# Attention over 1,024 tokens, one core: values left with channels on partitions, softmax sums inverted in a 128x16 tile and repeated by DMA, q and k stored in halves

## What is computed

```python
qkv = x @ w_qkv.T * hid ** (-0.5)
qkv = qkv.reshape(b, s, 3, heads, d)
...
scores = jnp.einsum('bhqd,bhkd->bhqk', q, k) * d ** (-0.5)
attn = jax.nn.softmax(scores, axis=-1) * (s / np.sqrt(s - 1.0))
out = jnp.einsum('bhqk,bhkd->bhqd', attn, v) * s ** (-0.5)
out = jnp.transpose(out, (0, 2, 1, 3)).reshape(b, s, hid)
return out @ w_o.T * hid ** (-0.5)
```

## Time and profile before

| | |
|---|---|
| median of 3 runs | 5755.92 us (5751.49 to 5757.47) |
| the profiled execution: time / span | 5750.62 us / 5748.9 us |
| busy in the span | PE 94%, DVE 78%, ACT 62%, POOL 26% |
| mean granted clock of TensorE | 0.976 of full speed |

### The profile page before, as it was taken

One profiled execution on the slowest core, in us unless ns is written; L12 is line 12 of the kernel. 1 busy time (PEld: TensorE's weight loads), 2 busy tenths in 40 slices (PEclk: granted clock), 3 DMA queues, 4 the chain that ended last, 5 costly groups with the idle time before them and its releaser, 6 DMA issues. The chain is left out here.

```text
span 5748.9 us, 131254 instructions
## 1 busy us (share of the span) xinstructions
PE 5428.0 (94%) x50092; PEld 3660.4 (64%) x50092; DVE 4498.2 (78%) x7377; ACT 3566.0 (62%) x5406; POOL 1473.5 (26%) x1948
## 2 busy tenths in 40 slices
PE   7999668999989889999999999999999997799999
PEld 6777457999978734444444444444444444699998
DVE  7888695555557689999999999999999996755554
ACT  5777562333325458888888888888888886433332
POOL 4655453333310000111111111111111114533332
PEclk9999889999999989999999999999999998999999
DMA  2222482222229811121112111111211113222221
GB/s 74 78 84 78 137 259 77 88 93 93 89 96 333 310 56 49 58 60 57 57 59 60 57 56 60 59 57 56 60 58 57 57 54 104 75 89 93 95 86 49
DMA packets 317697, 512.58 MB, mean 89 GB/s; under 512 B 36442, under 2 KB 221156, under 8 KB 311152
## 3 DMA queue, kind: packets, MB, share of 16 engines
q1 hardware_dynamic: 291912, 441.44, 24.2%
q0 software_dynamic: 24576, 64.56, 3.5%
q10 hardware_dynamic: 808, 1.07, 0.1%
HBM read 338.59 MB, written 185.60 MB: 91 GB/s over the span
## 5 line engine op out<-in xcount | busy, mean ns | idle before, releaser
L1773 DVE TENSOR_REDUCE at_best<-at_psM 128x2 f32<-128x1024 f32 x2048 | 2430.7, 1221 | 227.5 <-PE at_psM L1830 214.3
L1729 ACT ACTIVATE at_p<-at_psE 128x1024 f32<-128x1024 f32 (+1 forms) x2688 | 2077.1, 824 | 529.5 <-PE at_psE L1846 515.7
L1846 PE MATMUL at_psE<-at_q,at_k 50*128 50x512 f32 x4096 | 1174.0, 436 | 7.5 <-ACT at_p L1729 6.3
L1830 PE MATMUL at_psM<-at_k,at_q 48*128 48x512 f32 x4096 | 1093.6, 458 | 37.5 <-DMA at_k<-scratch_qk 27.4
L1857 PE MATMUL at_psO<-at_p,at_v 128*17 128x256 f32 x16384 | 1109.9, 383 | 0.1
L1122 ACT ACTIVATE e_h_hi<-e_psH 128x512 fp32r<-128x512 f32 x512 | 306.7, 599 | 916.0 <-PE e_psH L90 864.4
L1846 PEld LDWEIGHTS at_psE<-at_q,at_k 50*128 50x128 f32 x4096 | 548.7, 185 | 462.4 <-issue 223.6
L1196 DVE SCALAR_TENSOR_TENSOR e_h_lo<-e_psH,e_h_hi 128x512 fp32r<-128x512 f32 x512 | 353.9, 691 | 595.9 <-ACT e_h_hi L1122 505.8
L1857 PEld LDWEIGHTS at_psO<-at_p,at_v 128*17 128x17 f32 x16384 | 364.1, 96 | 542.7 <-issue 345.4
L1830 PEld LDWEIGHTS at_psM<-at_k,at_q 48*128 48x128 f32 x4096 | 471.3, 185 | 312.2 <-DVE at_best L1773 147.2
L90 PE MATMUL e_psE<-e_w_hi,e_h_hi 128*128 128x256 f32 x2048 | 583.1, 285 | 0.0
(11 more groups left out here) (213 smaller groups left out, 8456.5 us busy)
## 6 DMA issues: line engine op xcount, KB each, us to landing
e_w_raw<-in_w SPq DMA_DIRECT2D x64, 1024.0 KB
scratch_qk<-cp_qkh SPq DMA_DIRECT2D x64, 512.0 KB
scratch_qk<-cp_qkl SPq DMA_DIRECT2D x64, 512.0 KB
at_q<-scratch_qk SPq DMA_DIRECT2D x256, 128.0 KB
at_k<-scratch_qk SPq DMA_DIRECT2D x252, 128.0 KB
scratch_v<-cp_va SPq DMA_DIRECT2D x32, 544.0 KB
at_v<-scratch_v SPq DMA_DIRECT2D x126, 136.0 KB, 10.0
a_x<-in_x SPq DMA_DIRECT2D x32, 512.0 KB
```

The costliest lines, as they stand in the source:

```text
L1729: nc.scalar.activation(P[:, u:u + n, :], src, ACT.Exp, scale=HD ** -0.5).then_inc(p_ready, 1)
L1773: nc.vector.reduce_max(best[j % 2][:, h, :, qt], psM[h][:], AX_X).then_inc(m_taken, 1)
L1830: last = nc.tensor.matmul(psM[h][:, a, :], Q[j][r, 128 * qt:128 * qt + 128], K[j][r, 512 * h:512 * h + 512], start=True, stop=True)
L1846: last = nc.tensor.matmul(psE[:, u - u0 if n == 2 else 2, :], K[j][r, 128 * kc:128 * kc + 128], Q[j][r, 512 * half:512 * half + 512], star ...
```

## The change

- The DRAM tensor of q and k gets the two halves of the tokens as its first dimension. The loads of a pair take one kind of row at a time, 12 DMAs of 16 partitions where there were 8 of 32 or 16.
- `turn_values`, `normalise`, `turn_out` and `take_out` are gone. SP stores `at_oT` as it is to a DRAM tensor `scratch_ot`, moves its eight rows of sums into a tile `at_sums` of 128 x 16, DVE inverts that in place (`invert`), SP stores it (`scratch_rd`), and a unit is loaded back as 128 channels x 256 tokens (`at_raw`) beside its inverses repeated over 16 partitions (`at_den`). POOL multiplies the two before it splits.
- A unit is loaded at the start of a pair, but in pairs pb = 0 and pb = 4 behind `load_max` and `store_inverses`, since it needs the inverses of the pair just before.
- At the end of the stage the last four units are loaded with their sums repeated, inverted and multiplied on DVE.
- The PE order of a pair is written anew, and the maxima are turned at group 13 instead of 11.

```diff
@@ -1283,7 +1283,7 @@
     NG = N // G
     H, HD = 16, 16
     xg_ = x.rearrange("(b p u t) d -> u b p t d", u=2, p=128, t=4)
-    qkb = qk.rearrange("r (b h) d n -> b r (h d) n", h=H)
+    qkb = qk.rearrange("s r (b h) d n -> s b r (h d) n", h=H)
     vb = v.rearrange("b p s h k w -> s b p h k w")
     with ExitStack() as ctx:
         sb, ps, sem = tools(nc, ctx, stage)
@@ -1490,10 +1489,13 @@
     QROW, MROW = 48, 50
     NG = 21
...
+    xb = x.rearrange("(b p n) d -> b n p d", n=KC, p=128)
+    ob = out.rearrange("(b n p) d -> b n p d", n=KC, p=128)
+    qkp = qk.rearrange("s r (u a) d n -> u a r d s n", a=2)
     vp = v.rearrange("b p s (u x) k w -> u b p s (x k w)", x=2)
+    rows = ot.rearrange("(b k i) a (m w) c -> b k m (i a) w c", k=2, i=4, m=4)
+    inverses = rd.rearrange("x m i n -> x i m n")
+    inverse_rows = rd.rearrange("(b k) m i (a c) -> b k m (i a) c", k=2, a=2)
     with ExitStack() as ctx:
         sb, ps, sem = tools(nc, ctx, stage)
         Q = [sb(f"q{j}", [128, S], F32R) for j in range(4)]
...
         LEAD = 5
-        OUT_AT, MAX_AT, VALUES_AT, NORM_AT = 1, 11, 3, 3
+        OUT_AT, MAX_AT, VALUES_AT, INVERT_AT = 1, 13, 3, 11
 
...
                 r = 64 * a
-                eng.dma_start(Q[j][r:r + 32, :].bitcast(F32), row(qkp, pp)[a, 0:2]).then_inc(qk_loaded[j], 16)
-                eng.dma_start(Q[j][r + 32:r + 48, :].bitcast(F32), row(qkp, pp)[a, 0]).then_inc(qk_loaded[j], 16)
+                for n, kind in enumerate((0, 1, 0)):
+                    eng.dma_start(Q[j][r + 16 * n:r + 16 * n + 16, :].bitcast(F32), row(qkp, pp)[a, kind]).then_inc(qk_loaded[j], 16)
 
...
+            def store_values(p):
+
+                sp.wait_ge(oT_ready, p + 1)
+                T.settle(sp)
+                sp.dma_start(ot[p].rearrange("a r c -> r a c"), OT[:].rearrange("r (a c) -> r a c", a=2)).then_inc(oT_stored, 16)
+                if p < NP - 1:
+                    after(sp, rden_stored[p % 2], 16 * (p // 2))
+                    T.settle(sp)
+                    sp.dma_start(sums[p % 2][:], OT[HD:128:32, :].rearrange("q (w e) -> q w e", e=16)).then_inc(sums_moved, 16)
+
+            def store_inverses(p):
+
+                sp.wait_ge(rden_ready, p + 1)
+                T.settle(sp)
+                sp.dma_start(inverses[p // 4, p % 4], sums[p % 2][:]).then_inc(rden_stored[p % 2], 16)
+
+            def load_unit(u, slot, b, k, m, needed):
+
+                sp.wait_ge(oT_stored, 16 * needed)
+                T.settle(sp)
+                for s in range(2):
+                    sp.wait_ge(rden_stored[s], 8 * needed)
+                    T.settle(sp)
+                after(sp, ofT_ready, u - 1)
+                T.settle(sp)
+                sp.dma_start(raw[slot][:], rows[b, k, m][:, 0:HD, :]).then_inc(unit_loaded[slot], 16)
+                sp.dma_start(den[slot][:], inverse_rows[b, k, m].unsqueeze(1).broadcast_to([8, HD, 256])).then_inc(unit_loaded[slot], 16)
 
             load_queries(sp, 0, 0)
...
             def pair(pp, pb, b):
+                def next_unit():
+
+                    if has_turned(pp):
+                        u, k, m = turned_unit(pp, pb)
+                        load_unit(u, pb % 2, b if pb >= 4 else b - 1, k, m, PB * b + 4 if pb >= 4 else PB * b)
+
+                if pb % 4 > 0:
+                    next_unit()
                 if there(pp + 3):
                     after(sp, e_done, pp * NG)
                     T.settle(sp)
+                    load_queries(sp, pp + 3, (pb + 3) % 4)
+                    load_keys(sp, pp + 3, (pb + 3) % 4)
                     after(sp, pv_done, pp * KC)
                     T.settle(sp)
-                    load_pair(pp + 3, (pb + 3) % 4)
+                    load_values(sp, pp + 3, (pb + 3) % 4)
+                if not first(pp):
+                    store_values(pp - 1)
                 if there(pp + 1):
                     load_max(pp + 1, (pb + 1) % 4)
+                if not first(pp):
+                    store_inverses(pp - 1)
+                if pb % 4 == 0:
+                    next_unit()
                 if has_out(pp):
                     u, (ub, n) = out_unit(pp, pb, b)
                     store_out(u, ub, n)
             batches(pair)
+            store_values(NP - 1)
...
-                pool.wait_ge(xo_taken, u + 1)
+                pool.wait_ge(unit_loaded[slot], 32 * (u // 2 + 1))
+                T.settle(pool)
+                after(pool, xo_lo_ready, u - 1)
+                T.settle(pool)
+                nc.gpsimd.tensor_tensor(oT[slot][:], raw[slot][:], den[slot][:], ALU.mult).then_inc(ofT_ready, 1)
+                pool.wait_ge(ofT_ready, u + 1)
...
             def take_values(p):
                 act.wait_ge(pv_done, KC * p + KC)
-                after(act, t_done, p)
+                after(act, oT_stored, 16 * p)
+                after(act, sums_moved, 16 * p)
                 nc.scalar.activation(OT[:], psO[:], ACT.Copy).then_inc(oT_ready, 1)
-
-            def take_out(u, slot, bank):
-                act.wait_ge(xo_done, u + 1)
-                after(act, xo_lo_ready, u - 1)
-                nc.scalar.activation(oT[slot][:], bank[:, 128:384], ACT.Copy).then_inc(xo_taken, 1)
 
...
-            def normalise(p, pb, b):
-
-                dve.wait_ge(t_done, p + 1)
-                tv = psO[:].rearrange("p (a t w) -> p a t w", a=2, t=KC)
-                nc.vector.reciprocal(rden[:], tv[:, :, :, HD]).then_inc(rden_ready, 1)
-                dve.wait_ge(rden_ready, p + 1)
-                if pb % 4 == 0:
-                    after(dve, xo_taken, PB * b + pb - 4)
-                nc.vector.tensor_tensor(O[:, :, 32 * pb:32 * pb + 32].rearrange("p t (a d) -> p a t d", a=2), tv[:, :, :, 0:HD],
-                                        rden[:].unsqueeze(3).broadcast_to([128, 2, KC, HD]), ALU.mult).then_inc(o_ready, 1)
+            def invert(p):
+
+                dve.wait_ge(sums_moved, 16 * (p + 1))
+                nc.vector.reciprocal(sums[p % 2][:], sums[p % 2][:]).then_inc(rden_ready, 1)
+
+            def divide_end(m):
+
+                span = slice(256 * m, 256 * m + 256)
+                dve.wait_ge(end_loaded[m], 32)
+                nc.vector.reciprocal(end_den[:, span], end_den[:, span]).then_inc(end_rden_ready, 1)
+                dve.wait_ge(end_rden_ready, m + 1)
+                nc.vector.tensor_tensor(end_raw[:, span], end_raw[:, span], end_den[:, span], ALU.mult).then_inc(end_oT_ready, 1)
 
             for j in range(4):
...
                 if kc == 0 and heads[0] == 0:
-                    after(pe, o_ready, pp)
+                    after(pe, oT_ready, pp)
                     pe.wait_ge(v_loaded[j], 16 * (pp // 4) + 16)
...
-            def turn_values(p):
-
-                pe.wait_ge(oT_ready, p + 1)
-                for c in range(4):
-                    last = nc.tensor.transpose(psO[:, 128 * c:128 * c + 128], OT[:, 128 * c:128 * c + 128], T.ident[:])
-                last.then_inc(t_done, 1)
-
-            def turn_out(k, m, needed, bank):
-                pe.wait_ge(o_ready, needed)
-                for t in range(2):
-                    last = nc.tensor.transpose(bank[:, 128 + 128 * t:256 + 128 * t], O[:, 2 * m + t, 128 * k:128 * k + 128], T.ident[:])
-                last.then_inc(xo_done, 1)
...
-                def turns():
+                def next_max_rows():
 
                     pe.wait_ge(p_ready, NG * pp + MAX_AT - 1)
-                    if has_turned(pp):
-                        u, k, m = turned_unit(pp, pb)
-                        turn_out(k, m, PB * b + 4 if pb >= 4 else PB * b, psE[:, 2, :])
                     if there(pp + 1):
                         max_rows(pp + 1, (pb + 1) % 4)
 
-                output(), query(0, -1), key(0), last_values(6)
-                query(1, 0), query(2, 0), key(1), key(2), last_values(7)
-                key(3), query(3, 3), key(4)
-                if not first(pp):
-                    turn_values(pp - 1)
-                key(5), query(4, 5), query(5, 5), key(6), values(pp, pb % 4, 0)
-                key(7), query(6, 7), key(8), values(pp, pb % 4, 1)
-                key(9), query(7, 9), key(10), query(8, 10), turns(), values(pp, pb % 4, 2, (0,))
-                query(9, 10), key(11), key(12), values(pp, pb % 4, 2, (1,))
-                values(pp, pb % 4, 3, (0,)), query(10, 12), key(13), query(11, 13), key(14), values(pp, pb % 4, 3, (1,))
+                output(), query(0, -1), key(0), query(1, 0), last_values(6)
+                query(2, 0), key(1), key(2), last_values(7)
+                key(3), query(3, 3), query(4, 3), key(4), values(pp, pb % 4, 0)
+                key(5), key(6), query(5, 6), values(pp, pb % 4, 1, (0,))
+                key(7), query(6, 7), key(8), values(pp, pb % 4, 1, (1,))
+                query(7, 8), key(9), query(8, 9), key(10), values(pp, pb % 4, 2)
+                key(11), query(9, 11), key(12), query(10, 12), next_max_rows(), values(pp, pb % 4, 3, (0,))
```

(25 more changed lines are left out.)

47 lines of the change are left out of this document (24 added, 23 removed).

## The result

The changed kernel takes **5803.18 us** (median of 4 runs, 5801.53 to 5806.07) beside 5756.69 us of the kernel before on the same chip (4 runs, 5751.49 to 5758.22): a ratio of **1.0083**, 95% interval 1.0065 to 1.01. It is slower, 11 us above the predicted 5792. Its profiled execution has a span of 5801.1 us and a mean granted clock of 0.968, before 0.976.

A forecast was written before the change was run, and what follows sets the result against it. PE was taken to set the pace, with DVE close behind. 5750.6 - 70 (pairs) + 110 (stall and clock) - 12 (loads) + 8 (end) = 5786.6, with 5.3 us for the median 5792 us; range 5705 to 5865.

The forecast's parts named there:

- The late unit, pb = 1: Projection opening pairs pb = 1: PE stands 5.3 us for the unit, plus 2.0 us of low clock, 15 times, +110 us.
- Transposes off PE: PE's line in each pair: 0.86 us of transposes and at best a 0.30 us copy wait go, floor 20.16 us.
- What the new order gives back: Waits at three key groups and one query take back 0.6 us a pair; gain 0.55 us, -70 us over 128 pairs.
- Loads of q and k: Start of the attention stage: 16-row loads spread over more engines, so the first query comes sooner, -12 us.
- The end: End of attention, from ACT's copy to the first projection: some 11.5 us where it took 3.7, +8 us (5 to 12).
- SP, POOL: SP's longer line of issues is still free when `load_max` comes, and POOL's multiplies lie in its idle time.
- The unit in time: Rival: the late chain is 5 us shorter, so PE does not stand in pairs pb = 1; 5682 us, chance 0.1.
- The pairs at their floor: Rival: PE's line reaches 20.16 us a pair, gaining more than the stall takes; 5714 us, chance 0.2.
- The signs set down beforehand: Changed profile: 5 us projection gap in pairs pb = 1, clock 0.5 behind it, first query near 2011.5, DMA share near 0.5.

The follow-up runs named there:

- busy_stall: The changed kernel with 40 identity transposes on PE ahead of the projection in pairs pb = 1, while it waits for the unit: 5779.02 us, ratio 1.0045.
- unit_in_time: Changed kernel, inverse three or four maxima earlier, inverses' store and unit loads ahead of `load_max`, raw rows loaded before the wait for that store: 5692.76 us, ratio 0.9883.
- light_both: unit_in_time with maxima over half the keys and exponentials over half the queries, output not the reference's: pairs of 20.13 us, 5617.62 us.
- either light run: unit_in_time with only the maxima over half the keys (pairs 20.60 us, 5658.52 us), or only the exponentials over half the queries (20.55 us, 5662.67 us).
- layout_alone: The kernel before with only the new layout of q and k and its loads of 16 rows: 5742.31 us, ratio 0.9981.

## Why the prediction was right

- *The late unit, pb = 1.* Right in place, chain and count. The stand was sized at 5.3 us and is 6.1, the clock at 2.0 and is 1.9 (busy_stall), together 7.3 and 8.0 (unit_in_time): +110 predicted, +121 measured. The chain itself summed to a stand of 4.9; why 5.3 was taken the prediction does not say. Counted as in the prediction, from the start of the pair's projection (3082.59 in PE's timeline), `load_max` runs from 15.3 to 18.4 us (predicted 15.3 to 18.2), the unit's first load is issued at 20.6 (20.6), PE is done at 20.8 (20.8), and POOL begins at 25.0 where 23.6 was predicted. What was under-sized is the load of the inverses: 2.5 us from its issue on, where in the pair shown 3.7 lie between 3103.86 and POOL's start at 3107.59. The inverses' store took 2.1 us with its issue (3101.08 to 3103.19), 2.4 were set.
- *The Trainium skill's rule* ("TensorE: Matmul & The Clock Gate", "Why this matters for your kernels"), that gaps between bursts throttle the array, agrees with the 0.50 in the windows above and with the 28.6 us of busy_stall.
- *Transposes off PE.* The floor of 20.16 us agrees with the 20.13 of light_both, but in part by luck, since its parts were off in opposite ways: 0.68 for the transposes and not 0.86, and 0.50 of waits in the pair before, not 0.30. The 1.3 us of waits that the prediction read from the loads in the earlier trace rows are too many: all waits of the pair before are 0.50. Nor is the 0.30 us for ACT's copy seen in PE's starts: in the kernel before, the transposes start 0.49 us behind the two keys ahead of them (3020.22 and 3020.71), and values start 0.56 behind two such (3010.70 and 3011.26).
- *What the new order gives back.* The size was right, 0.6 against 0.62 us measured; the cause was wrong, so the size was luck. I laid the waits to the new order; with the old one they are 0.96. Removing the transposes uncovers them, and the new order takes a third back. Both VectorE and ScalarE hold them, as either light run alone shows. The prediction laid them at three key groups and one query; which places they are was not looked up. A pair gains 0.58 us, -74 in all, against -70.
- *Loads of q and k.* -12 predicted, -11 in the rows and -12 by layout_alone. The Trainium skill's rule of the slowest dimension of both sides ("DMA: Bandwidth & Descriptors", "Why a DMA increments its semaphore by 16 and not by 1") fits: the first query comes 10.8 us sooner in layout_alone. The number and the size of the loads and the layout of the projection's stores changed with it, so it is not shown that this rule alone is the cause. "Nothing waits for it there" was true of the kernel before alone; on the new path, in unit_in_time, the old loads cost 725 us, a link between two parts of the change that I had not priced.
- *The end.* +8 predicted, +12 measured, at the upper end of its range. The +8 was counted to the first projection, and there it is 8.6. The other 3.6 us lie behind it, where the prediction had nothing. I priced the reciprocal like that of 128x16; over 128x256 it takes 1.75 us, four times on VectorE, with the first projection behind the second. The granted clock is lower there too: 0.59 from 4836 to 4842.5, where it was 1.00 from 4789.9 to 4796.5 before.
- *SP, POOL.* Hidden, as said, except where SP's queue makes the unit late.
- *The rivals.* The unit in time was given 5682 us; built, it takes 5693. The pairs at their floor would need 0.62 us of waits gone; neither of the two orders run here removes them.

The signs set down beforehand came: the projection idle for about 6 us behind POOL's subtraction, half clock behind it, the first query at 2013.62 (said: near 2011.5, from a stage that began 0.57 us sooner), the undisturbed pair 20.73 us, a clock of 0.98 in the middle, and a DMA share of 0.53 from 3084 to 3086, while SP issues loads of q and k. The total came out 11 us under the 5803 because the late unit had 11 too little, the end 4 and the start 1, against 4 too little of gain in the pairs.

## What to carry to other kernels

A path through DRAM costs an engine nothing until one of its links stands in a queue behind something unrelated: count from the last input to the first reader, and put the queue's order first; here two moved blocks and an inverse placed three or four maxima earlier turned 1.008 into 0.988. Work taken off the bounding engine is worth what the next engines let through, and two of them can hide each other, so lighten both before naming one. Before adding small transfers on which something waits, measure how long they take to land behind the big ones.
